# Moving the first pair's weight products into the gaps between the first head stacks

## The reference

```python
x = layernorm(x + attn(x))           # latent q and kv (64), 16 heads of 16, half of it rotated
x = layernorm(x + xattn(x, ctx_512)) # 16 heads over 512 context rows of width 64
x = layernorm(x + ffn(x))            # 8 experts, top 2, and a shared one
```

```python
q_hk   = hidden_q @ Wq.T                  # per head 128 wide
q_big  = q_hk[h] @ w_kc_q[h]              # 192 wide
q_r    = q_big @ W_qr[h]                  # 64 wide
k_r    = kv_rope @ W_kr[h]
scores = q_r @ k_r.T
```

## Time and profile before

| | |
|---|---|
| median of 3 runs | 255.16 us |
| the profiled execution | 255.44 us |
| its span, from the first to the last instruction | 253.7 us |
| TensorE busy | 238.6 us, 94% |
| VectorE busy | 194.2 us, 77% |
| ScalarE busy | 120.6 us, 48% |
| GpSimd busy | 119.8 us, 47% |
| mean granted clock of TensorE | 0.993 |

### The profile page before, as it was taken

How to read it: one execution, slowest core, us unless ns; L and a number is a source line. 1 busy time by engine, 2 the same in 40 slices (tenths; PEclk the granted TensorE clock), 3 DMA queues, 4 the chain that set the end, 5 groups by cost and what they waited for, 6 DMA issues and landing times.

```text
span 253.7 us, 4411 instructions
## 1 busy us (share of the span) xinstructions
PE 238.6 (94%) x1581; PEld 172.7 (68%) x1581; DVE 194.2 (77%) x348; ACT 120.6 (48%) x253; POOL 119.8 (47%) x170
## 2 busy tenths in 40 slices
PE   7989999978999999999899999999999999999991
PEld 4468797755656557675667776668776777778870
DVE  1377578799874899769889999995857895886685
ACT  2555358655566355454366554454344434513360
POOL 7297300000025528757666666784465646502353
PEclk9999999999999999999999999999999999999997
DMA  6999970000000660000000000000000000000002
GB/s 240 331 268 264 402 281 0 4 1 3 0 3 1 123 125 3 0 0 0 4 0 0 4 0 0 4 0 0 3 0 0 0 4 0 0 3 0 0 3 83
DMA packets 4501, 13.66 MB, mean 54 GB/s; under 512 B 513, under 2 KB 1281, under 8 KB 4353
## 3 DMA queue, kind: packets, MB, share of 16 engines
q1 hardware_dynamic: 4048, 11.29, 13.8%
q0 software_dynamic: 432, 2.10, 3.8%
HBM read 14.43 MB, written 0.52 MB: 59 GB/s over the span
## 4 chain that ended last, share of the span: by engine, by line
PE 70%; DVE 16%; DMA 5%; issue 2%; ACT 2%; SPq 2%; POOL 1%; POOLq 0%
PE ps L854 10%; PE ps L807 6%; PE ps L868 5%; PE ps L834 5%; PE ps L835 5%; PE ps L808 5%; DMA wq<-in_wq 5%; PE ps L791 5%; DVE rcp L1332 3%; PE ps L934 3%; PE ps L647 3%; DVE mneg L1361 3%; PE ps L841 2%; DVE xmneg L1423 2%; PE ps L709 2%
## 5 line engine op out<-in xcount | busy, mean ns | idle before, releaser
L1195 ACT ACTIVATE probs<-ps 128x512 f32<-128x512 f32 x64 | 38.0, 597 | 57.0 <-PE ps L835 56.0
L1423 DVE TENSOR_REDUCE xmneg<-ps 128x1 f32<-128x512 f32 x64 | 43.1, 688 | 18.0 <-PE ps L808 17.7
L454 POOL TENSOR_TENSOR psums<-psums,probs 128x512 f32<-128x512 f32 x32 | 41.2, 1287 | 11.2 <-ACT probs L1195 8.5
L450 POOL TENSOR_TENSOR psums<-probs 128x512 f32<-128x512 f32 x16 | 20.5, 1281 | 34.2 <-ACT probs L1195 22.6
L807 PE MATMUL ps<-KA,QA 128*128 128x512 f32 x64 | 30.1, 470 | 2.1 <-DVE xmneg L1423 2.1
L854 PE MATMUL ps<-probs,kv_dup 128*64 128x256 f32 x256 | 31.1, 385 | 0.0
L1441 DVE RECIPROCAL xrcp<-ps 128x256 f32<-128x256 f32 x16 | 28.0, 1751 | 1.1 <-PE ps L841 1.0
L1361 DVE TENSOR_REDUCE mneg<-ps 128x4 f32<-128x1024 f32 x16 | 19.6, 1224 | 9.5 <-PE ps L587 9.1
L834 PE MATMUL ps<-QA,KA 128*128 128x512 f32 x64 | 26.0, 406 | 0.0
L398 POOL TENSOR_TENSOR rstd<-mv,eps_col 128x1 f32<-128x1 f32 x12 | 2.3, 188 | 49.5 <-DVE mv L1349 49.2
L835 PE MATMUL ps<-QB,KB 68*128 68x512 f32 x64 | 25.4, 397 | 0.0
(11 more groups left out here) (163 smaller groups left out, 464.1 us busy)
## 6 DMA issues: line engine op xcount, KB each, us to landing
wu<-in_wu SPq DMA_DIRECT2D x4, 640.0 KB, 9.8
wq<-in_wq SPq DMA_DIRECT2D x4, 512.0 KB, 13.9
wcT<-in_wcT SPq DMA_DIRECT2D x4, 384.0 KB, 12.6
wE<-in_wE SPq DMA_DIRECT2D x4, 320.0 KB, 11.5
w13T<-in_w POOLq DMA_DIRECT2D x1, 1024.0 KB, 7.8
x1T<-in_xT SPq DMA_DIRECT2D x1, 512.0 KB, 3.7
kvp<-in_kv POOLq DMA_DIRECT2D x1, 512.0 KB, 6.1
x_nat<-in_xn SPq DMA_DIRECT2D x1, 512.0 KB, 19.6
```

What stands on the lines that cost most here:

```text
L454: g.tensor_tensor(psums[:, s, :], psums[:, s, :], probs[:, s, kc, :], ALU.add).then_inc(xadd_sb, 1)
L1195: a.activation(probs[:, n % 2, kc, :], ps[:, 2 + u % 2, :], ACT.Exp).then_inc(xexp_sb, 1)
L1423: v.tensor_reduce(xmneg[:, n % 4, qt, hh:hh + 1], ps[:, u % 2, :], AX.X, ALU.max, negate=True).then_inc(xmax_sb, 1)
```

## The change

Pair 0's E and G leave their places behind the second stack. E(0) takes the place of three of the six fillers ahead of the first stack, in bank 0, where the stack will write; the three that stay go to bank 1. The stack waits for ScalarE's copy of E(0). G(0) takes the place of four of the six fillers ahead of the second stack, in bank 4, once the first `half_out` has read it; values(0), which also writes bank 4, now waits for the copy of G(0). ScalarE's copies move with them: E(0)'s ahead of `half_out(0)`, G(0)'s ahead of the QS copy. Behind the second stack there remain E(1) and values(0), now in this order. The three tensors of each weight group get a semaphore each: step E of a group's first pair waits for wE alone, its step G for wcT, its step M for wq. The order in which the transfers are issued stays as it was.

```diff
-        ld_wg = [sem(f"ld_wg{g}") for g in range(4)]
+        ld_wE = [sem(f"ld_wE{g}") for g in range(4)]
+        ld_wc = [sem(f"ld_wc{g}") for g in range(4)]
+        ld_wq = [sem(f"ld_wq{g}") for g in range(4)]
...
-                sp.dma_start(wE[:, pairs, :], wE_in[:, pairs, :]).then_inc(ld_wg[g], 16)
-                sp.dma_start(wcT[:, hs], wcT_in[:, hs]).then_inc(ld_wg[g], 16)
-                sp.dma_start(wq[:, hs, :], wq_in[:, hs, :]).then_inc(ld_wg[g], 16)
+                sp.dma_start(wE[:, pairs, :], wE_in[:, pairs, :]).then_inc(ld_wE[g], 16)
+                sp.dma_start(wcT[:, hs], wcT_in[:, hs]).then_inc(ld_wc[g], 16)
+                sp.dma_start(wq[:, hs, :], wq_in[:, hs, :]).then_inc(ld_wq[g], 16)
...
+        def E_bank(p):
+            return 0 if p == 0 else 5
+
+        def G_bank(p):
+            return 4 if p == 0 else 6
...
             def values(t0):
                 if t0 == 0:
-                    pe.wait_ge(half_sb, 1)
+                    pe.wait_ge(G_out, 1)
...
-            keep_busy(6, 0)
+            def step_E(p):
+
+                if p % 2 == 0:
+                    pe.wait_ge(ld_wE[p // 2], 16)
+                if p == 1:
+                    pe.wait_ge(rot_sin, 1)
+                if p >= 1:
+                    pe.wait_ge(E_out, p)
...
+            def step_G(p):
+
+                pe.wait_ge(E_out, p + 1)
+                if p % 2 == 0:
+                    pe.wait_ge(ld_wc[p // 2], 16)
+                if p == 0:
+                    pe.wait_ge(half_sb, 1)
+                if p == 1:
+                    pe.wait_ge(half_sb, 2)
...
+            step_E(0)
+            keep_busy(3, 1)
             pe.wait_ge(spread_sb, 1)
+            pe.wait_ge(E_out, 1)
             stack_tiles(0, range(4), 0)
             pe.wait_ge(half_sb, 1)
-            keep_busy(6, 4)
+            keep_busy(2, 4)
+            step_G(0)
             pe.wait_ge(stack_act, 1)
             pe.wait_ge(stack_dve, 1)
             stack_tiles(1, range(4), 0)
...
+            def step_M(p):
+
+                pe.wait_ge(G_out, p + 1)
                 if p % 2 == 0:
-                    pe.wait_ge(ld_wg[p // 2], 48)
...
+                    pe.wait_ge(ld_wq[p // 2], 16)
...
-            step_E(0)
+            step_E(1)
             values(0)
-            step_E(1)
-            step_G(0)
...
+            step_E(0)
             half_out(0)
             stack_out(0, 1, slice(0, 2), 0)
             half_out(1)
+            step_G(0)
             stack_out(1, 2, slice(0, 2), 0)
...
-            step_E(0)
             step_E(1)
-            step_G(0)
```

More of the change, by code:

```diff
@@ L550, in stack_tiles @@
                 mm.then_inc(stack_ps, 1)
-            keep_busy(6, 0)
+            def step_E(p):
[5 more added lines that the diff above has]
+                    pe.wait_ge(E_out, p)
+                for c in range(2):
+                    mm = pe.matmul(ps[0:96, E_bank(p), c * P:(c + 1) * P], wE[:, p, P + 96 * c:P + 96 * c + 96], wE[:, p, 0:P],
+                                   start=True, stop=True)
+                mm.then_inc(E_ps, 1)
+            def step_G(p):
[6 more added lines that the diff above has]
+                    pe.wait_ge(half_sb, 2)
+                if p >= 1:
+                    pe.wait_ge(G_out, p)
+                for k in range(2):
+                    for c in range(2):
+                        mm = pe.matmul(ps[:, G_bank(p), DC * k:DC * k + DC], wcT[:, 2 * p + k, c, :], E_sb[:, p % 2, c, DC * k:DC * k + DC],
+                                       start=(c == 0), stop=(c == 1))
+                mm.then_inc(G_ps, 1)
+            step_E(0)
+            keep_busy(3, 1)
             pe.wait_ge(spread_sb, 1)
+            pe.wait_ge(E_out, 1)
             stack_tiles(0, range(4), 0)
             pe.wait_ge(half_sb, 1)
-            keep_busy(6, 4)
+            keep_busy(2, 4)
+            step_G(0)
             pe.wait_ge(stack_act, 1)
@@ L670, in context_T @@
                 mm.then_inc(kvT_ps, 1)
-            def step_E(p):
-                if p % 2 == 0:
-                    pe.wait_ge(ld_wg[p // 2], 48)
[L676 to L696, removed]
             def step_M(p):
                 pe.wait_ge(G_out, p + 1)
+                if p % 2 == 0:
+                    pe.wait_ge(ld_wq[p // 2], 16)
                 if p == 0:
@@ L1087, in rotated_hi, with step_E, step_G @@
                 a.activation(dhi[:, kq, 1, :], dense[:, kq, 1, :], ACT.Copy).then_inc(hi_sb, 1)
+            def step_E(p):
+                act.wait_ge(E_ps, p + 1)
+                if p >= 2:
+                    act.wait_ge(G_ps, p - 1)
+                a.activation(E_sb[:, p % 2].rearrange("p a b -> p (a b)"), ps[0:96, E_bank(p), 0:2 * P], ACT.Copy).then_inc(E_out, 1)
+            def step_G(p):
+                act.wait_ge(G_ps, p + 1)
+                if p >= 2:
+                    act.wait_ge(M_ps, p - 1)
+                a.activation(G_sb[:, p % 2, :], ps[:, G_bank(p), 0:P], ACT.Copy).then_inc(G_out, 1)
+            step_E(0)
             half_out(0)
@@ L1107, in attn_sums_out @@
                 a.activation(sums[:], ps[:, 4, SEQ:2 * SEQ], ACT.Copy).then_inc(sums_sb, 1)
[L1109 to L1119, removed]
             def step_M(p):
```

## The result

The changed kernel took 254.65 us, the median of 20 runs (254.03 to 256.11), against 255.46 for the kernel before, run beside it; the ratio is 0.9969, with a 95% interval of 0.9957 to 0.9981. So it is faster by 0.3%, about 0.8 us. 253.7 had been forecast, with a gain of 1.44. Of the 0.95 us between 253.7 and 254.65, 0.3 is the kernel before, whose median was 255.16 in the three runs that the forecast started from and is 255.46 in these 20; the rest is gain that did not come. Two of these 20 runs (272.16 and 592.79 us), and in the experiments three more of the kernel before (262.9 to 264.9 us, mean clock 0.958 to 0.972), one of e9 (274.36) and one of e10 (264.69), lie far above the others and are left out of the ratios and counts, though not of the medians.

The account below looks back on a forecast made before the run. TensorE's stream and a weight transfer were taken to bound the head. The terms -0.52 - 0.93 - 0.21 + 0.22 = -1.44 us at E(2), carried to the end, took the median from 255.16 to 253.7 us, range 253.1 to 254.9.

Parts of the forecast that it names:

- The removed slots: Behind the head stacks, one E slot (0.52 us) and the G slot (0.93 us) leave TensorE's stream ahead of E(2).
- the stall: At 17.91 us, E(2)'s wait for the wq load, 0.21 us of TensorE idle time, goes with per-tensor semaphores.
- the new wait: Ahead of the first stack, TensorE waits for ScalarE's copy of E(0): 0.22 us lost, at most 0.6.
- the switch from values(0) to the maximum: Behind values(0) in the head, taken as 1.05 us from its nearest row, 0.1 to 0.2 either way.
- its gap: Ahead of the second stack, two fillers and G(0) fit before the KS copy ends, with some 0.2 us spare.
- as the prediction said of the semaphores: At E(2), with the group's old condition it would still start at 17.9 us and the gain be nothing.
- Rivals B and C: First: E(2) still meets a transfer, 255.2 us, chance 0.05. Second: E(0) waits for weights ahead of the first stack, 0.05.
- the step from E(2) to the end: After E(2), no clock-time event binds TensorE, so the whole 1.44 us shift reaches the kernel's end.
- The prediction's own sign of it: After E(2), TensorE idle time appearing between 16.5 and 38.6 us would show the prediction wrong.
- Rival A: G(0) overruns its gap, the switch is dearer, or VectorE's head becomes late; gain 0.5 to 1.2 us, chance 0.27.
- rival D: TensorE's clock falls to 1.2 GHz in the head, 11.20 to 17.91 us; about 259.5 us, chance 0.03.

Follow-up runs that it names:

- e9: e6 with E(0) between the two pairs of up matmuls and two fillers instead of three behind them; median 254.22 us, ratio 0.9943.
- e10: Kernel before, with GpSimd's second-batch rotation waiting for VectorE's split of the first maxima, plus sixteen fillers in attention rounds 5 and 6; median 255.47 us, ratio 1.0005.
- e1: Kernel before with one semaphore for each weight tensor and nothing moved; median 255.17 us, ratio 0.9989.
- e11: Changed kernel with the old whole-group weight waits, and twelve fillers where TensorE waits for wq; median 255.77 us, ratio 1.001.
- e5: Changed kernel with GpSimd's rotation of the second batch's context waiting for VectorE's split of the first two maxima; median 254.24 us, ratio 0.9955.
- e7: Changed kernel with only E(0) moved to the front, G(0) staying behind the second stack; median 254.96 us, ratio 0.9986.
- e3: Changed kernel with sixteen more fillers, eight each at the ends of attention rounds 5 and 6; median 254.33 us, ratio 0.9952.
- e4: Kernel before with sixteen more fillers, eight each at the ends of attention rounds 5 and 6; median 255.38 us.
- e6: Changed kernel with both the GpSimd wait of e5 and the sixteen fillers of e3; median 253.76 us, ratio 0.9937.
- e8: e6 with E(0) one step earlier, ahead of the fourth up matmul; median 254.76 us, ratio 0.9972.
- e12: e6 with eight more fillers where TensorE waits for the cross attention's maxima near 117 and 119 us; median 253.70 us, ratio 0.9915.
- e2: Changed kernel with E(2), E(4) and E(6) waiting for all three weight tensors of their group again; 263.23 us, ratio 1.0284.

## Why the prediction was wrong

Right were these steps. The removed slots, the stall and the new wait, 1.44 in all, measured 1.67 at E(2) against the profiled run, 1.39 against e1, which has no stall. The difference to 1.67 is mostly the switch from values(0) to the maximum (0.17) and the stall, which was worth 0.28, and not the 0.21 that TensorE's row shows as idle. The forecast wait at the first stack, 0.22, measured 0.25 (3.11 us from the first up matmul instead of 2.86), of which TensorE's row shows 0.19 as idle. G(0) fitted its gap by 0.27 us, 0.2 forecast, and the second stack came at 13.65, 13.6 forecast. The switch from values(0) to the maximum, kept at 1.05 for want of a row, was 0.88. E(2) met no transfer. The finer semaphores alone give nothing (e1) and the moves alone nothing (e11), so the gain needs both, as the prediction said of the semaphores. Rivals B and C did not occur.

Wrong was the step from E(2) to the end: "Nothing that TensorE needs after it is pinned to a clock time near enough to bind", and with it "so the shift is carried to the end". The prediction's own sign of it came: TensorE idle for 0.27 us at 23.79, between 16.5 and 38.6. The step failed twice in the profiled execution; without the two losses the shift does reach the end (E(2) to the end 235.7 to 235.8 in both orders).

First, I asked of GpSimd's work only whether its results are in time, and they were, by many microseconds. What binds is that the instructions are there at all: they hold up VectorE's, and VectorE's split moved 1.4 us forward into them. It cost 0.33 us in the profile, and 0.43 by the fastest runs (e5). Rival A, with a gain of 0.5 to 1.2 us, holds the measured 0.8, and its chance was 0.27; but none of its causes occurred as it gave them: G(0) fitted, the switch was cheaper and not dearer, and VectorE's head was late because GpSimd held it up, not because it gains less than TensorE. So the number of rival A came by luck, and so did the place of 254.65 inside the stated range, 253.1 to 254.9.

Second, rival D looked at the clock in the head only, with a chance of 0.03, for less filler. In the profiled execution the clock fell elsewhere: behind a wait of 1.07 us in the attention rounds (in e11 also behind one of 0.81 us near 121), which the change does not touch. In the profiled execution this took 1.34 - 0.63 = 0.71 us. What it takes of the medians is not shown. A mean clock of 0.990 or below tells of an interval before the last one, since the last one takes at most 0.008 off the mean in the profiles; at 0.991 to 0.993 the clock does not tell. By this mark 6 of 20 runs of the changed kernel have one, and 29 of 95 of the kernel before: the same share. The changed kernel has 14 of 20 runs more than 0.5 us above its fastest, but two of these have mean clocks of 0.998 and 0.999, and six more are at 0.991 to 0.993. So it is not shown that the new order meets intervals more often.

What the fillers do shows in the same count. Of the kernels without them (before, after, e1, e5, e7, e11) 47 of 163 runs are at 0.990 or below, of those with the sixteen (e3, e4, e6, e8, e9, e10, e12) 7 of 70. The old order alone has 3 of 23 (e4, e10). There the medians don't move, for only a third of its runs had an interval to lose. In the new order they fall by 0.32 (e3 against after) and 0.48 us (e6 against e5, six runs). That the idle time of 1.07 us brought the clock down at 56 us is likely, by e2 against e11 and by this count, but was not shown by itself: the kernel before waits as long there and keeps its clock.

The sum that would have been right for the profiled execution: -1.67 at E(2), +0.33 for VectorE against GpSimd and +0.71 for the clock give -0.63; the spans, known to 0.1 us, differ by 0.7. For the medians, which differ by 0.8, -1.39 to -1.67 and +0.33 leave 0.25 to 0.5 us. Half-rate intervals and the start of the head are what the runs offer for it; how much each takes stays open.

## What to carry to other kernels

When work of one engine is moved in time, ask of the others not only whether their results are ready, but what they will then be running beside it: here a cast of 128 x 8 numbers took VectorE 0.7 us because GpSimd was at work. In a stream with idle times of about a microsecond the fastest run can show a gain that the median has only in part, because of the clock; with cheap matmuls in those idle times fewer runs had a half-rate interval (7 of 70 against 47 of 163). To compare two profiles, count from an event behind the loads and not from the span's start: here the loads alone move the head by up to 1 us. Before a wait is added to TensorE's stream, price it twice: its length, and what it does if the clock falls behind it.

## What the runs showed of the hardware

- One idle time of 1.31 us, in a stream that had been busy but for 0.5 us in the 6 us before it, was followed by 17 us at the 1.2 GHz level, although TensorE was busy without a gap in them (e2); one of 1.07 us by 3.6 us at a mean of 0.53 (after). Idle times of 1.08 and 1.23 us in the kernel before were followed by no fall. Twelve bf16 matmuls of 128x256 in the first, 1.3 us of work, kept the clock at 1.00 (e11).
- The 17 us ended at about 35 us, just behind the first eight bf16 fillers of that stretch (32.59 to 34.26). The rest of it held float32 matmuls with weights loaded for each. What in it kept the clock low the runs don't tell.
- Two float32 matmuls of 64 rows and 512 columns, in rows 0 to 63 and 64 to 127, take 0.96 us together (1.92 for two pairs in the kernel before) and 1.05 us one alone (e8); a pair with E(0) behind it takes 1.06 (e9). The Trainium skill (page "TensorE: Matmul & The Clock Gate", section Why this matters for your kernels) says that matmuls in distinct row groups run concurrently; the trace agrees, and adds that a matmul of another shape put between the two costs a further 1.05 us.
